# Cross-attention and mixture of experts on one core: the router's logits taken from two products that exist already, and all row maxima subtracted on GpSimd

## The reference, cut to what matters

```python
qh, kh, vh = proj(layernorm(x), Wq, bq), proj(ctx, Wk, bk), proj(ctx, Wv, bv)
scores = einsum('bhqd,bhkd->bhqk', qh, kh)
scores = alpha * 4 * scores / (norm_q[..., :, None] + norm_k[..., None, :]) ** 2
x = x + merge_heads(softmax(scores) @ vh) @ Wo + bo
y = layernorm(x)
logits = y @ Wr                      # 8 experts
w, idx = top_k(softmax(logits), 2); w = w / w.sum()
x = x + sum over the 2 experts of w * (gelu(y @ W1[e] + b1[e]) @ W2[e] + b2[e])
```

## Time and profile before

| | us |
|---|---|
| median of 3 runs (917.53 to 922.07) | 920.61 |
| the profiled execution | 916.38 |
| its span | 914.6 |
| PE busy | 865.5 (95%) |
| DVE busy | 648.8 (71%) |
| ACT busy | 590.1 (65%) |
| POOL busy | 451.6 (49%) |

### The profile page before, as it was taken

One profiled execution on the slowest core, in us unless ns is written; L12 is line 12 of the kernel. 1 busy time (PEld: TensorE's weight loads), 2 busy tenths in 40 slices (PEclk: granted clock), 3 DMA queues, 4 the chain that ended last, 5 costly groups with the idle time before them and its releaser, 6 DMA issues. The chain is left out here.

```text
span 914.6 us, 30058 instructions
## 1 busy us (share of the span) xinstructions
PE 865.5 (95%) x10189; PEld 756.1 (83%) x10189; DVE 648.8 (71%) x2566; ACT 590.1 (65%) x1205; POOL 451.6 (49%) x509
## 2 busy tenths in 40 slices
PE   3899999999999999999888999999999999999993
PEld 2678887887877877788667899999999999999993
DVE  6667788787877778787876777876666666666662
ACT  2588787887888878877675556555555555555551
POOL 7445666759667596676554422442222232222222
PEclk9899999999999999999988999999999999999997
DMA  6212323223222443253333963443333333333221
GB/s 160 71 32 89 95 70 111 63 95 125 72 87 92 140 155 114 88 163 118 124 114 115 373 186 55 108 91 53 52 50 49 52 52 50 51 54 50 43 25 24
DMA packets 61892, 84.78 MB, mean 93 GB/s; under 512 B 9872, under 2 KB 55312, under 8 KB 59568
## 3 DMA queue, kind: packets, MB, share of 16 engines
q1 hardware_dynamic: 47504, 64.26, 22.3%
q0 software_dynamic: 13296, 18.00, 11.6%
q10 hardware_dynamic: 944, 0.60, 0.3%
HBM read 49.86 MB, written 31.92 MB: 89 GB/s over the span
## 5 line engine op out<-in xcount | busy, mean ns | idle before, releaser
L1616 POOL DMA_INDIRECT out<-yw,rb x71 | 110.7, 1559 | 262.7 <-DVE yw L1415 234.7
L956 ACT ACTIVATE h<-s_ps,b1t,inv 128x128 f32<-128x128 f32 x288 | 104.4, 468 | 89.2 <-PE s_ps L719 88.4
L956 ACT ACTIVATE h<-u_ps,b1t,inv 128x128 f32<-128x128 f32 x280 | 101.4, 468 | 84.5 <-PE u_ps L719 84.5
L1398 DVE TENSOR_SCALAR hs<-h,hsc 128x512 f16<-128x512 f32 x142 | 69.8, 491 | 105.7 <-ACT h L956 104.3
L1132 DVE CUSTOM_DVE_ANT_0 tw<-th,s_ps 128x128 f32<-128x128 f32 x512 | 111.4, 281 | 35.8 <-issue 23.7
L849 ACT ACTIVATE pt<-gen,escale 128x512 f32<-128x512 f32 x128 | 86.9, 680 | 40.1 <-PE gen L509 34.7
L1400 DVE SCALAR_TENSOR_TENSOR hs<-h,hsc,hs 128x512 f16<-128x512 f32 x142 | 106.7, 752 | 5.1
L719 PE MATMUL s_ps<-xt,w1s 128*128 128x128 f16 x1728 | 103.3, 220 | 0.0
L1569 POOL DMA_INDIRECT xrec<-rec,idx x64 | 72.1, 1126 | 61.6 <-DVE idx L1249 46.0
L739 PE MATMUL pv_ps<-w2s_sb,hs 128*128 x864 | 100.2, 273 | 0.3 <-issue 0.3
L719 PE MATMUL u_ps<-xt,w1s 128*128 128x128 f16 x1680 | 99.5, 219 | 0.4 <-issue 0.4
(11 more groups left out here) (243 smaller groups left out, 1657.5 us busy)
## 6 DMA issues: line engine op xcount, KB each, us to landing
wl<-L_ffn_W SPq DMA_DIRECT2D x16, 1024.0 KB, 6.5
rb<-xrec SPq DMA_DIRECT2D x71, 132.5 KB, 2.1
w2s<-wst SPq DMA_DIRECT2D x8, 1024.0 KB, 9.0
w2s_sb<-w2s SPq DMA_DIRECT2D x8, 1024.0 KB, 6.4
xin<-x SPq DMA_DIRECT2D x32, 128.0 KB, 2.3
cin<-ctx SPq DMA_DIRECT2D x32, 128.0 KB, 2.3
xres<-x SPq DMA_DIRECT2D x32, 128.0 KB, 2.3
out<-x SPq DMA_DIRECT2D x30, 128.0 KB, 2.3
```

The costliest lines, as they stand in the source:

```text
L956: ins = act.activation(h32[n % HBANKS][:, m % HB, :], hbank[n % HBANKS][:, o:o + SLOT], ACT.Gelu, scale=inv1[:, bass.ds(ex, 1)].bitcast(F3 ...
L1398: dve.tensor_scalar(hi, h, scale, None, ALU.mult).then_inc(sig("hi"), 1)
L1616: pool.indirect_dma_start(out[:, :], bass.IndirectOffsetOnAxis(ap=rb[j][:, D + NE:D + NE + 1], axis=0), yw[s % 2][:, :], None, compute_op= ...
```

## The change

It has five parts.

1. **All maxima on POOL.** `take_max` (after.py, 1581) subtracts the maximum from the 128x1024 tile in all four groups. PE's small matmuls of line 509 and POOL's split of the maximum are gone, and `turned` waits for `ml` in every group.
2. **Key turned unpadded.** POOL no longer writes `ku`. PE transposes the copied key directly, two transposes in place of four, into the same bank as the query's. ACT then writes it twice, each time with a 0/1 scale per partition (`mine`), which makes the zeros.
3. **Logits as columns.** Wr less its column mean is put ahead of Wq (8 more columns, 264 in place of 256), and Wo times that matrix behind Wo (also 264). The logits are then the sum of a query column times the standard deviation (`first_logits` on DVE, kept in `la`) and an output column (an added operation in `residual`). PE's `turn_y` and `logits`, ACT's copy `xn2t` and DVE's `logits` are gone. The difference of the two best logits is multiplied by the second norm's factor, one more operation on DVE. At the start there are new products, transposes and copies that make the two matrices.
4. **Layer norms on POOL.** The mean is negated first by an operation on one column (`less`), and the 128x256 pass has the form (x + less) * rstd in place of (x - mean) * rstd. The first norm also makes `std1`, one more operation on one column.
5. **Projection and banks.** `project` makes key and value first, in one bank, and query last, in the bank before it. The bank of each user stands in the table. Apart from these, each engine's order of calls is as it was.

```diff
-    ("xct0", 1, "xce0", None), ("qk0", 1, "qke0", None), ("v0", 1, "ve0", None), ("ex00", 0, "ex00", None),
+    ("xct0", 1, "xce0", None, 0), ("kv0", 1, "qke0", None, 1), ("q0", 1, "qke0", None, 0), ("ex00", 0, "ex00", None, 2),
...
             def project(b, p):
-                pe.wait_ge(*at(f"xce{b}", p + 1))
-                g = pe_turn(pe, f"qk{b}", p)
+                g = pe_turn(pe, f"kv{b}", p)
...
-                pe.matmul(g[:, :], ones_b[0:RROWS, :], bqp[:, :], start=True, stop=False)
-                for k in range(DC):
-                    pe.matmul(g[:, 0:D], xct[b][:, k, :], wq_sb[:, k, :], start=False, stop=False)
+                pe.matmul(g[:, 0:D], ones_b[0:RROWS, :], bqp[:, NE + D:NE + 2 * D], start=True, stop=False)
                 pe.wait_ge(*dma(f"ldc{b}_{p % 2}", p // 2 + 1))
                 for k in range(DC):
-                    ins = pe.matmul(g[:, D:2 * D], cin[b][:, p % 2, k, :], wk_sb[:, k, :], start=False, stop=(k == DC - 1))
+                    pe.matmul(g[:, 0:D], cin[b][:, p % 2, k, :], wk_sb[:, k, :], start=False, stop=(k == DC - 1))
+                for k in range(DC):
+                    ins = pe.matmul(g[:, D:2 * D], cin[b][:, p % 2, k, :], wv_sb[:, k, :], start=(k == 0), stop=(k == DC - 1))
+                ins.then_inc(sig(f"v{b}"), 1)
+                g = pe_turn(pe, f"q{b}", p)[:, D - NE:2 * D]
+                pe.wait_ge(*at(f"xce{b}", p + 1))
...
+                pe.matmul(g, ones_b[0:RROWS, :], bqp[:, 0:NE + D], start=True, stop=False)
+                for k in range(DC):
+                    ins = pe.matmul(g, xct[b][:, k, :], wq_sb[:, k, :], start=False, stop=(k == DC - 1))
                 ins.then_inc(sig(f"qk{b}"), 1)
...
                 for k in range(2):
-                    for odd in range(2):
-                        o = (2 * k + odd) * P
-                        src = ku[b][:, k, odd, :, :, :].rearrange("p g s d -> p (g s d)")
-                        ins = pe.transpose(g[:, o:o + P], src, idf[:, :])
+                    src = qk[:, b, NE + D + k * P:NE + D + (k + 1) * P]
+                    ins = pe.transpose(g[:, (2 + k) * P:(3 + k) * P], src, idf[:, :])
...
                 if i == 0:
-                    pe.wait_ge(*at(f"ml{n}" if h else f"tm{n}", p + 1))
+                    pe.wait_ge(*at(f"ml{n}", p + 1))
                 g = pe_turn(pe, f"ex{n}{i}", p)
                 for j in range(4):
...
-                    for j in range(4):
-                        for part in range(2):
-                            m = mhl[:, part, 4 * i + j:4 * i + j + 1].to_broadcast([P, P])
-                            ins = pe.matmul(g[:, j * P:(j + 1) * P], m, negb[:, :], start=False, stop=(j == 3 and part == 1))
+                    ins = pe.transpose(g[:, j * P:(j + 1) * P], tw[h][:, i, j, :], idf[:, :])
...
-                pool.tensor_scalar(xn[b][:, :], xin[b][:, :], mv[:, 0:1], rstd[:, :], ALU.subtract,
+                pool.tensor_scalar(xn[b][:, :], xin[b][:, :], less[:, :], rstd1[b][:, :], ALU.add,
                                    ALU.mult).then_inc(sig(f"xn{b}"), 1)
...
+            def first_logits(b, p):
+                dve.wait_ge(*at(f"qke{b}", p + 1))
+                dve.wait_ge(*at(f"sd{b}", p + 1))
+                dve.scalar_tensor_tensor(la[b][p % 2][:, :], qk[:, b, 0:NE], std1[:, p % 3, b:b + 1], brc[:, :], ALU.mult,
+                                         ALU.add).then_inc(sig(f"la{b}"), 1)
```

More of the change, by code:

```diff
@@ L151, in build @@
     pv_ps = bank("pv_ps", [P, 512], F32)
-    gen = [bank(f"gen{i}", [P, 512], F32) for i in range(3)]
+    gen = bank("gen", [P, 3 * 512], F32)
     def turn(what, p):
-        return gen[bank_of[place[what, p]]]
+        i = bank_of[place[what, p]]
+        return gen[:, i * 512:(i + 1) * 512]
     def bank_free(bank, end):
@@ L194, in build @@
     b1ss = alloc(ctx, "b1ss", [P, NE], F32)
-    lm_bufs = [[alloc(ctx, f"lm{b}_{k}", [P, w], F32) for k, w in (("st6", 6), ("mv", 2), ("var", 1), ("rstd", 1))]
+    lm_bufs = [[alloc(ctx, f"lm{b}_{k}", [P, w], F32) for k, w in (("st6", 6), ("mv", 2), ("var", 1), ("less", 1))]
                for b in range(2)]
@@ L226, in build @@
         stats = lambda stack, name: [[alloc(stack, f"{name}{b}_{k}", [P, w], F32) for k, w in
-                                      (("st6", 6), ("mv", 2), ("var", 1), ("rstd", 1))] for b in range(2)]
+                                      (("st6", 6), ("mv", 2), ("var", 1), ("less", 1))] for b in range(2)]
+        rstd1 = pair(a, "rstd1", [P, 1], F32)
+        std1 = alloc(a, "std1", [P, 3, 2], F32)
         norm_bufs = {"ln": stats(a, "ln")}
-        qk = alloc(a, "qk", [P, 2, 2 * NH, DK], F32)
+        qk = alloc(a, "qk", [P, 2, NE + 2 * D], F32)
         qk2 = alloc(a, "qk2", [P, 2, 2 * NH, DK], F32)
         qu = pair(a, "qu", [P, NH, DK], F32)
-        ku = pair(a, "ku", [P, 2, 2, 4, 2, DK], F32)
+        head_no = alloc(a, "head_no", [P, 1], I32)
+        mine = [alloc(a, f"mine{odd}", [P, 1], F32) for odd in range(2)]
         n2 = alloc(a, "n2", [P, 2, 2 * NH], F32)
@@ L349, in sync_program @@
                 if it == -4:
-                    sp.wait_ge(*at("set_pool", 4))
-                    for i in range(TWO):
-                        row = NE * REGION + i * P
-                        sp.dma_start(xrec_d[row:row + P, :], padrec[:, :]).then_inc(sig("set_pad"), 16)
-                    sp.wait_ge(*at("set_dve", 2))
-                    sp.dma_start(out[T:T + P, :], zrow[:, :]).then_inc(sig("set_pad"), 16)
+                    store_pads()
             def load_records(s):
@@ new lines, in fold_bias @@
+            def fold_bias():
+                pe.wait_ge(*at("set_wom", 1))
+                for k in range(DC):
+                    pe.matmul(pv_ps[:, 400:400 + NE], pt[1][:, 1, k * P:(k + 1) * P], wq_sb[:, k, 0:NE], start=(k == 0), stop=False)
+                for k in range(DC):
+                    ins = pe.matmul(pv_ps[:, 400:400 + NE], bv_sb[:, k:k + 1].to_broadcast([P, P]), wo_sb[:, k, D:D + NE],
+                                    start=False, stop=(k == DC - 1))
+                ins.then_inc(sig("set_fold"), 1)
@@ L1343, in vector_program @@
                     residual(1, it - 2)
-                    logits(0, it - 2)
                 if 0 <= it - 1 < NP:
```

339 lines of the change are left out of this document (181 added, 158 removed), and 14 rows, old and new, of the table TURNS.

## The result

The changed kernel takes **932.28 us** (median of 4 runs, 927.18 to 936.22) against 919.5 for the kernel before (4 runs, 917.53 to 922.07): a ratio of 1.0124, 95% interval 1.0095 to 1.0153. It is slower, and the forecast of 928 with its likeliest range of 925 to 936 held. The sum behind it did not hold: it put +6 into the middle of the attention part and +1.7 into the start; the traces show it the other way round.

A forecast was written before the change was run, and what follows sets the result against it. PE was taken as the attention part's bound, busy 372 of 378 us. Pairs +6, start +0.9 and +0.8, last pair +1.5, expert part -1.4: together +8 on 916.4, plus 0.5%, 928 us; range 905 to 950, likeliest 925 to 936.

The forecast's parts named there:

- PE loses 3.6 us per pair and little of it comes through: Attention pairs: PE work falls 3.6 us per pair, of which 0.8 comes through from rows transposes to next first-group transposes.
- P to R gets longer, 5.3 and 6.3: From first group's transposes to rows transposes: 5.3 us in place of 4.44, and 6.3 in place of 5.39, in alternate turns.
- POOL and DVE get in each other's way: Before rows transposes: DVE's first norms operation waits for POOL's two subtractions of 1.90 us, ending 3.7 after first group's transposes.
- late turn: Every second pair, where first group's transposes follow five scatters; rows transposes forecast 6.3 us after them, in place of 5.39.
- early turn: The other pairs: rows transposes forecast 5.3 us after first group's transposes, in place of 4.44; POOL blocks nothing.
- The norm pass, 0.61: POOL's 128x256 norm pass in the new form: 0.61 us in place of 1.23, saving 0.62 per pass.
- R to P, 23.45 by ACT's chain: Rows transposes to next pair's first-group transposes: 23.45 us, set by ACT's exponentials and the query's wait for ex31's bank.
- The clock falls in one pair of four, at 1.2 us: Behind rows transposes, idle PE brings half clock: 1.2 us in one pair of four, 0.6 per two pairs.
- Start +1.7: Kernel start: query last +0.9 us; six more transposes and a 768-column copy, mostly hidden by a DMA wait, +0.8.
- The last pair +1.5, the expert part -1.4: Kernel end: two subtractions without next-pair work to hide them, +1.5 us; logits and transposes leaving the expert part, -1.4.
- signs that I had named: Attention part: PE below 92% busy, named waits on PE, first-group to rows transposes over 5 us, norms operation ending with POOL's subtraction.
- rival 2: Whole kernel: gains and losses cancel, no change that can be told, 916 to 925 us; chance 0.25.

The follow-up runs named there:

- e4: Changed kernel with GpSimd's norm passes back in the old form, the added small operations left in: 929.4 us, ratio 1.0086 to the kernel before.
- e5: Kernel before with only GpSimd's norm pass changed to the faster form with the negated mean: 920.92 us, ratio 0.9986.
- e12: Same kernel as e9, run again in another set: 913.32 us, ratio 0.9916 to the kernel before.
- e2: Changed kernel with products nobody reads in PE's waits for the norms ahead of the rows transposes: 924.95 us, ratio 1.0052 to the kernel before.
- e1: Changed kernel with DVE's rounding of the biases ahead of its wait for the router's column sums: 927.06 us, ratio 1.0082 to the kernel before.
- e7: Changed kernel with biases rounded first, unread products in PE's norm and first key-row waits, GpSimd's fills held until that rounding: 917.78 us, ratio 0.9960.
- e11: e5 with GpSimd's fills at the start held back until DVE has rounded the biases: 926.55 us, ratio 0.9959 to the kernel before.
- e6: Kernel before with products nobody reads in PE's waits at the first two rows transposes: 922.68 us, ratio 1.0010.
- e9: e7 with the banks of group 3's two halves exchanged, no instruction moved: 919.83 us, ratio 0.9886 to the kernel before.

## Why the prediction came out, and where it was wrong

**PE loses 3.6 us per pair and little of it comes through**: right in kind, too large in size. By the profile's busy time PE loses 2.7 us per pair in two undisturbed pairs (57.26 to 51.93), and 0.3 per pair comes through.

**P to R gets longer, 5.3 and 6.3**: wrong in sum. It is 4.39 behind the five scatters and 5.47 in the other turn, 9.86 together against 9.83 before and 11.6 forecast. The step that failed is "POOL and DVE get in each other's way" in the late turn. I let GpSimd start the two subtractions at P + 1.1. That cannot be: P is PE's transposes of group 0, and they wait for the first of the two subtractions (`pool_max`, second place of the change). If GpSimd comes late, P comes late with it, and the lock can last at most one subtraction, until about P + 1.9. In the trace they begin 2.0 us before P (291.19):

```profile
289.24 3.75 POOL L1586 TENSOR_TENSOR tw<-tw,tm 128x1024 f32<-128x1024 f32 x2
```

They end at 292.99, and DVE's first norms operation takes 0.23 at 293.19. It is not the cheaper pass that does this: e4, with the slow one, also begins them 2.0 us before P (280.24 and 282.19), and there PE waits 1.56 us for them. So a late GpSimd lengthens R to P, and not P to R. For the early turn the steps as written (squares at P + 0.2, 2.12 to the norms, a wait of 0.2, 2.98 of norms) give P + 5.5, not the 5.3 that I added up, and 5.5 was measured. In that turn the lock does strike, from another side: the norms' last steps run beside GpSimd's `xn` and `qu`, and one cast takes 0.53:

```profile
265.04 0.56 POOL L1562 TENSOR_SCALAR xn<-xin,ln_less,rstd 128x256 f32<-128x256 f32 x1
...
265.70 0.53 DVE L1148 CAST ar<-na_r 128x64 bf16<-128x64 f32 x1
```

**The norm pass, 0.61**: measured 0.55 in e5 and in the changed kernel (medians; blocked ones are longer). The estimate of 0.38 by the Trainium skill, GPSIMD Engine Reference, section 3.1, lay below that, and the measurement decides.

**R to P, 23.45 by ACT's chain**: measured 23.72 and 24.07, so 0.3 to 0.6 more. The wait for `ex31` is there (12.8 us in 13 times over 62:440), and e12 shows that it costs. But e12 and e4 show a second chain through GpSimd's subtractions right beside it, which I had only behind P.

**The clock falls in one pair of four, at 1.2 us**: two of twelve, at 1.4 us (e2 takes back 3.05). Right within what two falls can tell.

**Start +1.7**: wrong, and this is the step that mattered: +18.2. I took "six more transposes and a copy of 768 columns ahead of the first scores, of which a DMA wait hides most, +0.8 (bounds 0 and 4)". It left out four things that were in the change or in the rows. The rounding of the biases stands behind DVE's new wait for the column sums, and the first projection needs it (e1: first R 5.1 us earlier, the kernel 3.9 to 5.2 us faster). GpSimd's faster passes start its fills while DVE casts (e4, e5, e7 and e11 show it from four sides). And I applied the price of an idle PE, to the pairs alone, where waits are 1.8 us, and not to the start, where they are 5.1 (e2: 7.3 us, of which 3.05 in the middle). The wait for `ex31`, which I counted from pair to pair, was also in the first periods (e12: 1.5 us).

**The last pair +1.5, the expert part -1.4**: the period 14 to 15 is 1.6 us shorter, the part behind it 1.1 shorter.

So +8 was forecast as +6 (middle, 15 pairs; +5 for twelve), +1.7 (start), +0.1 (end), and +16.7 came as +1.2 (twelve), +18.2 and -2.7. The call and the range held by luck: an overestimate of the middle and of the end stood in for part of a start that I had not costed, and the medians differ by 12.8 where the traces differ by 16.7. Of the signs that I had named, PE's share (89.8%), the waits ahead of R and P and the query's wait for the exponential came; P to R above 5 us in both turns, and a norms operation that ends with GpSimd's second subtraction, did not. With the start mended (e7) the change is 0.4% faster than the kernel before, which is my rival 2.

## What to carry to other kernels

Cost the first iteration by itself: it has no other work to hide behind, a wait there can cost clock as well, and a new wait placed ahead of old set-up work delays all of that. A faster operation on an engine that shares ports with another moves everything behind it, so ask whom it now meets. And when the bound engine is relieved, expect several chains of nearly equal length: here 2.7 us less on PE per pair gave 0.3, and two edits off PE (e11) gave the same ratio as the whole change with a mended start (e7).

## What the hardware showed that I had not expected

- On GpSimd, (x - mean) * rstd over 128x256 takes 1.22 to 1.24 us, and (x + negated mean) * rstd takes 0.55. The small operation that negates costs 0.19 alone, and up to 2.2 beside a DVE operation over 128x2048; in the kernel before, the `pow` that stood there took up to 2.6.
- DVE casts and copies with one input, some of them of a single row of 512, took 1.2 to 2.7 us in place of 0.3 to 0.5 beside GpSimd's fills, and ended up to 0.6 us behind them.
- Products that nobody reads, placed in waits, made a kernel 0.7% faster (e2 against the change, by the ratios), and gave nothing in another (e6).
- One kernel on two chips (e9 and e12) took 4.0 us more over twelve middle periods on the one, and the kernel before a median of 930.7 there and not 921, with every kind of instruction as long and the waits longer. Ratios can be compared across sets only with care.
